# A normalised graph network: where ScalarE squares a pair of kept copies in its statistics pass

## What is computed

```
D = jnp.abs(x[:, :, None, :] - x[:, None, :, :])
h = jnp.einsum('bijc,oc->bijo', D, W1) + b1
m = jnp.mean(h, axis=(0, 1, 2))
v = jnp.mean((h - m) ** 2, axis=(0, 1, 2))
h = (h - m) / jnp.sqrt(v + EPS) * g1 + be1
s = jnp.einsum('bijo,uo->biju', _leaky(h), W2)[..., 0] + b2[0]
A = jax.nn.softmax(jnp.where(A_init > 0, s, NEG), axis=-1)
y = _leaky(norm(jnp.einsum('bij,bjc->bic', A, x) @ Wg.T + bg))
out = jnp.concatenate([x, y], axis=2) @ Wt.T + bt
```

## Time and profile before

| | us |
|---|---|
| median of 3 runs | 2326.1 (2325.75 to 2334.32) |
| the profiled execution | 2333.18 |
| its span, first to last instruction | 2330.9 |
| statistics pass, ScalarE's first square to the last copies | 380.9 to about 1609 |

### The profile page before, as it was taken

The page is one execution under the profiler, slowest core; times in us unless marked ns, Lnnn a source line. Parts: engine busy times, 40 slices in busy tenths (PEclk is TensorE's granted clock), DMA queues, the critical chain, the costliest instruction groups (busy, mean ns, idle before and its releaser), DMA issues.

```text
span 2330.9 us, 35023 instructions
## 1 busy us (share of the span) xinstructions
PE 1995.3 (86%) x12741; PEld 799.4 (34%) x12741; DVE 2120.4 (91%) x2647; ACT 2165.3 (93%) x2988; POOL 43.2 (2%) x50
## 2 busy tenths in 40 slices
PE   5777777899999898989889899996899999999976
PEld 4555553333333333333333333332222222222226
DVE  5888868999999999999999999998999999999966
ACT  5999987999999999999999999996999999999975
POOL 0000000000000000000000000000000000000000
PEclk8999988999999999999999999998999999999997
DMA  4111104444444444444444444443899989989962
GB/s 122 42 42 42 42 15 149 183 182 180 190 182 181 185 181 184 186 184 177 185 174 185 180 180 190 176 186 156 341 349 354 354 347 357 352 340 354 352 242 73
DMA packets 221280, 470.49 MB, mean 202 GB/s; under 512 B 52344, under 2 KB 143288, under 8 KB 196536
## 3 DMA queue, kind: packets, MB, share of 16 engines
q1 hardware_dynamic: 220048, 467.91, 53.1%
q10 hardware_dynamic: 1064, 0.36, 0.1%
HBM read 254.25 MB, written 213.91 MB: 201 GB/s over the span
## 4 chain that ended last, share of the span: by engine, by line
ACT 42%; issue 23%; PE 13%; DMA 10%; DVE 9%; SPq 4%; ACTq 0%; POOLq 0%; POOL 0%; DVEq 0%
ACT hcopy L625 8%; ACT habs L625 8%; ACT yt L630 8%; ACT diff L613 7%; DMA ring_scores<-sring 4%; DVE ring L1085 4%; ACT habs L657 3%; PE banks L784 3%; PE banks L870 3%; PE banks L955 2%; DMA hcopy<-kept 2%; DMA diff<-kept 2%; ACT banks L635 2%; PE banks L794 2%; SPq L453 2%
## 5 line engine op out<-in xcount | busy, mean ns | idle before, releaser
L870 PE MATMUL banks<-diff,w1t 128*64 128x512 f32 x5136 | 1207.8, 603 | 122.0 <-ACT hcopy L625 57.0
L1213 DVE TENSOR_TENSOR diff<-ring 128x2048 f32<-128x2048 f32 x352 | 802.4, 2287 | 42.1 <-PE banks L870 42.1
L870 PEld LDWEIGHTS banks<-diff,w1t 128*64 128x64 f32 x5136 | 346.7, 137 | 855.3 <-issue 808.3
L1227 DVE TENSOR_SCALAR diff<-diff 128x2048 int32<-128x2048 int32 x354 | 418.2, 1220 | 0.0
L1353 DVE TENSOR_TENSOR diff<-ring 128x2048 f32<-128x2048 f32 x128 | 292.5, 2285 | 17.6 <-PE banks L870 17.4
L613 ACT ACTIVATE diff<-banks 128x2048 f32<-128x2048 f32 x128 | 238.5, 1863 | 2.8 <-PE banks L885 2.8
L955 PE MATMUL banks<-habs,w2s 128*32 128x512 f32 x816 | 159.1, 600 | 55.0 <-ACT hcopy L657 22.4
L630 ACT ACTIVATE yt<-hcopy,par 128x2048 f32<-128x2048 f32 x96 | 192.5, 2005 | 3.1
L630 ACT ACTIVATE yt<-habs,par 128x2048 f32<-128x2048 f32 x96 | 192.4, 2005 | 3.1
L625 ACT ACTIVATE hcopy<-banks 128x1024 f32<-128x1024 f32 x192 | 193.8, 1018 | 0.6 <-PE banks L870 0.6
L625 ACT ACTIVATE habs<-banks 128x1024 f32<-128x1024 f32 x192 | 193.7, 1018 | 0.3 <-PE banks L870 0.3
(11 more groups left out here) (215 smaller groups left out, 1929.0 us busy)
## 6 DMA issues: line engine op xcount, KB each, us to landing
kept<-hcopy SPq DMA_DIRECT2D x192, 512.0 KB, 2.9
kept<-habs SPq DMA_DIRECT2D x192, 512.0 KB, 2.9
hcopy<-kept SPq DMA_DIRECT2D x78, 1024.0 KB, 8.1
diff<-kept SPq DMA_DIRECT2D x76, 1024.0 KB, 8.3
habs<-kept SPq DMA_DIRECT2D x38, 1024.0 KB, 8.4
yt<-xrows SPq DMA_DIRECT2D x512, 40.0 KB, 2.0
adjt<-in_adj_dram SPq DMA_DIRECT2D x32, 256.0 KB, 2.8
diff<-in_x_dram SPq DMA_DIRECT2D x32, 128.0 KB, 2.1
```

What stands on the lines that cost most here:

```text
L870: last = nc.tensor.matmul(dst[half * O:(half + 1) * O, bank * BANK:(bank + 1) * BANK], w1t[:, :], src[:, m * BANK:(m + 1) * BANK], start=T ...
L1213: v.tensor_tensor(shaped(diff[:, c % ND, :]), xj, xi_, ALU.subtract).then_inc(sub_done, 1)
L1227: v.tensor_scalar(bits, bits, ABS_BITS, None, ALU.bitwise_and).then_inc(abs_dve, 1)
```

## The change

The pair's square leaves sum_h and becomes square_pair(n), with the same operands and the same wait. It is called one turn of the loop later, behind the next chunk's sum_h. The pair that ends with chunk 15 is squared behind chunk 0 of the next element, and the last pair of all behind the loop.

```diff
--- before.py
+++ after.py
@@ -623,26 +623,37 @@
                     if n >= KB:
                         act.wait_ge(kept_stored[n % KB], 16 * (n // KB))
                     nc.scalar.activation(tokeep[n % KB], h, ACT.Identity, accum_out=column(ODDS + n)).then_inc(kept_copied, 1)
-                    if n % 2:
-                        both = hcopy if n % KB < 4 else habs
-                        src = both[:, n % 4 - 1:n % 4 + 1, :].rearrange("p q n -> p (q n)")
-                        act.wait_ge(kept_copied, n + 1)
-                        nc.scalar.activation(spare, src, ACT.Square, bias=par[:, 53:54],
-                                             accum_out=column(SQUARES + B * NR + n // 2)).then_inc(sq_kept, 1)
                 else:
                     if c == 0:
                         act.wait_ge(shift_ready, 1)
                     nc.scalar.activation(h, h, ACT.Square, bias=par[:, 53:54],
                                          accum_out=column(SQUARES + b * NR + REDONE.index(ORDER[j]))).then_inc(sq_redone, 1)
 
+            def square_pair(n):
+
+                both = hcopy if n % KB < 4 else habs
+                src = both[:, n % 4 - 1:n % 4 + 1, :].rearrange("p q n -> p (q n)")
+                act.wait_ge(kept_copied, n + 1)
+                nc.scalar.activation(spare, src, ACT.Square, bias=par[:, 53:54],
+                                     accum_out=column(SQUARES + B * NR + n // 2)).then_inc(sq_kept, 1)
+
+            def pair_ends_at(b, j):
+
+                return j >= 0 and ORDER[j] not in REDONE and (b * NK + kept_before(j)) % 2 == 1
+
             absolute(0, 0)
             for b in range(B):
                 for j in range(CHUNKS):
                     sum_h(b, j)
+                    if pair_ends_at(b, j - 1):
+                        square_pair(b * NK + kept_before(j - 1))
+                    if j == 0 and b:
+                        square_pair(b * NK - 1)
                     if j + 3 in PE_AT:
                         absolute(b, j + 3)
                     if j + 3 == CHUNKS and b + 1 < B:
                         absolute(b + 1, 0)
+            square_pair(B * NK - 1)
             act.wait_ge(st_small, 11)
             nc.scalar.activation(par[:, 36:37], par[:, 35:36], ACT.Sqrt).then_inc(st_act, 1)
             act.wait_ge(st_small, 15)
```

## The result

The changed kernel takes **2479.7 us** (median of 6 runs, 2471.9 to 2486.5) against 2328.6 for the kernel before on the same runs: a ratio of 1.065, 95% interval 1.0626 to 1.0674. It is slower, by 151 us. The forecast was 2456 and the range 2438 to 2512. The sign and the places held, and the time lies in the range; the forecast is 24 us too low. 2 to 3 us of that are the kernel before itself, whose median went from 2326.1 to 2328.6 with more runs. The other 21 are the subject of half of the experiments.

The account below looks back on a forecast made before the run. ScalarE was taken to bound the statistics pass. From 2326.1 us, 28.7 saved on squares and 158.7 added by four stalls in each element gave 2456 us, range 2438 to 2512.

Parts of the forecast that it names:

- The bound: Statistics pass: ScalarE, busy 38.17 of 38.36 us an element, sets the pace; a microsecond on it is 32 us of the run.
- The saving: Pair squares on ScalarE: 191 no longer wait for the copy just ahead, 0.15 us each, 28.7 us saved.
- the idle time of the groups: Idle time before pair squares, 3.1 us for each of two buffers: 6.2 us, the low bound of the time saved.
- the estimate of 17.8 us: Pair squares on ScalarE: only the instruction overlap of about 93 ns won back, 191 x 0.093 = 17.8 us saved.
- The stall: ScalarE before chunks 3, 6, 9 and 12: waits 1.24 us for TensorE, 128 times, 158.7 us added.
- The sum of both terms: Whole run: 28.7 us saved and 158.7 us of stalls, 130.0 us added, giving 2456 us, 5.6% slower.
- VectorE and the stores: Statistics pass: VectorE's 37.07 us an element adds no wait, with two microseconds to spare; stores keep their order, further apart.
- The clock: TensorE in the pass: clock expected at 1.00, with nothing added to the forecast time for a fall.
- the list of signs: Expected in the pass: ScalarE about 90% busy, 1.24 us gaps before chunks 3, 6, 9, 12, elements 42.4 apart, clock 1.00.
- Rival 2: TensorE's gap before chunk 3: clock falls, 32 x 1.53 = 49 us, 2505 us (14%); all four gaps, 2652 us (5%).
- The sum's own upper bound: Whole run: 171.5 us of longer stalls less only 6.2 us saved, 2491 us.
- Rival 1: Statistics pass: TensorE is ahead anyway, so ScalarE only wins its 28.7 us, 2297 us, faster; chance 3%.

Follow-up runs that it names:

- the kernel with a single stall: Against the kernel before, only the square of the pair (1, 2) stands one instruction further down: 2363.5 us, ratio 1.015.
- the kernel with the filled gap: The changed kernel plus two unread matmuls, one into each half of PSUM's rows, in TensorE's gap before chunk 3 of each element: 2457.6 us, ratio 1.0555.
- the kernel with the saving alone: Against the kernel before, each square keeps its place behind a pair's second copy but squares the pair before: 2304.1 us, ratio 0.9888.
- the first filling: The changed kernel plus two unread matmuls, both into the same 64 rows of PSUM, in TensorE's gap before chunk 3: 2478.9 us, ratio 1.0643.

## Why the prediction was right, and where it fell short

**The bound.** That ScalarE sets the pass, and that a microsecond on it in each element is 32 of the run, held in every kernel here.

**The saving.** 0.15 for each square was forecast, 28.7 us; the kernel that does only this gained 26.4, and the one with two moved pairs 10.9 for 9.6. The difference of starts was the right measure, and not the idle time of the groups (6.2 us), which leaves out the lost overlap. The kernel before shows both parts in the reads of the accumulator behind the copies of chunks 1 and 2:

```profile
808.42 0.20 ACT L625 ACTIVATION_READ_ACCUMULATOR habs<-banks 128x1 f32 x1
...
809.42 0.21 ACT L625 ACTIVATION_READ_ACCUMULATOR habs<-banks 128x1 f32 x1
```

The first ends at 808.62, 0.10 us after the next copy has begun (808.52); the second ends at 809.63, 0.04 us before the square begins (809.67). So some 0.10 us of overlap is lost and the engine then idles for 0.03 to 0.04. The Trainium skill's 93 ns for the overlap (ScalarE: Activation LUTs, "What ACT_TABLE_LOAD costs") agrees with the first part; the estimate of 17.8 us from it alone is too low, since it leaves out the second, and the measured 26.4 us decides for the rows.

**The stall.** Forecast were 3.24 us from the start of a copy to the moment at which the next chunk in the same half can be read, and so 1.24 us with only one copy between. The trace has 3.26, and the kernel with a single stall took 35.1 us more, for 34.9. Four places in an element, and not six: the two last pairs have no stall. The sum of both terms was 130.0; the kernel with the filled gap measured 129.2.

**VectorE and the stores.** No wait of ScalarE in the pass ends on them, as forecast. The prediction had the kernel with the saving alone at 37.46 us an element, still over VectorE's 37.07; it came to 37.56, and the 0.10 was a wait for TensorE's chunk 11 and not for VectorE.

**The clock.** This is the term that was mis-sized: the sum put it at nothing, and the list of signs had the clock at 1.00, where the pass shows 0.98. Rival 2 had the place (the gap before chunk 3, 2.29 us) and the cause, but a chance of 14%, and only as all or nothing: 32 falls of 1.53 us, 49 us, or none. What came is a share of them, 20 of 31, at 1.1 us each, 22 us. The sum's own upper bound, 2491, covers the measured time by luck: it allowed for longer stalls and a smaller saving, and neither came. The argument against rival 2, that TensorE would be busy for 82% of an element where the attention pass keeps a full clock with 73%, compared means over many microseconds: in the kernel with only the fourth pair moved, TensorE is busy for 1064.40 of 1200 us, 89% (its slow chunks add to that), and the clock falls behind 30 of 31 gaps. The row that should have had the weight was the one in the scoring pass, a gap of 2.38 us with a slow chunk behind it; the gap to come was 2.29, and the longest without a fall in the rows 2.01. The forecast belonged between 2456 and 2505, and the range did reach over that.

**Rival 1** (faster) did not happen: a second half of PSUM helps only as far as ScalarE has other work between two uses of a half, and in this order that is one copy of 1.00 us where 3.24 are needed from copy to copy.

## What to carry to other kernels

With two buffers, the engine that empties them needs other work between two emptyings for as long as a refill takes; here 3.24 us from copy to copy, so a long instruction that seems to be in the way may be the cover. To get rid of an engine's wait for its own last result, exchange **what** the instruction works on (the pair before) and not its place in the order. And add up the gaps of TensorE that an order makes, not only ScalarE's: here a gap that grew from 1.7 to 2.3 us was paid a second time, behind 20 of 31.

## What the runs showed of the chip

- Behind gaps of 1.71 us (the kernel before, the run with the first pair) and 1.84 us (the last two pairs) in TensorE's work, 31 in each pass, no chunk was slow. Behind 31 gaps of 2.28 us (the changed kernel) 20 were, behind 31 of 2.89 us (the first four pairs) 22, behind 31 of 2.79 us (the fourth pair alone) 30. A slow chunk took between 2.4 and 3.6 us in place of 1.94. What decides behind which gaps the clock falls stays open; the length alone it is not, as the last two show.
- Work whose result nobody reads can pay: 64 added matmuls made the changed kernel 22 us faster.
- Two matmuls of 512 columns take 1.08 us together if they go to different halves of the rows of PSUM (the run with both halves). Into the same half they took 1.9 us (the first filling), and the chunk's result came 0.64 us later.
- A ScalarE instruction that waits for the result of the one just ahead starts 0.14 to 0.15 us later than one whose wait is long met: 1.15 us behind it and not 1.00 in the kernel before, and 26.4 / 191 = 0.14 us by the time of the kernel with the pair before.
